# A decoder layer whose feed-forward tail writes its output feature-major, with the last permutation done by indirect DMA

## The reference, cut to what matters

```python
x = x + _L0_attn_ref(_layernorm(x), ...)    # Mamba-like block: 8 groups, 128 heads of 64, inner width 8192
x = x + _L0_xattn_ref(_layernorm(x), ctx)   # fake-quantised product: q1 (256x512) @ q2 (512x512) per sequence
x = x + _L0_ffn_ref(_layernorm(x), up, down, perm)
```

## Time and profile before

| | |
|---|---|
| time, median of 3 runs | 809.83 us (809.65 to 810.01) |
| the profiled execution | 810.87 us |
| its span in the trace | 809.0 us |
| TensorE busy | 787.9 us (97%) |
| VectorE, ScalarE, GpSimd busy | 712.9, 548.3, 589.1 us |
| DMA | 111.14 MB, mean 137 GB/s |

### The profile page before, as it was taken

One profiled execution on the slowest core, in us unless ns is written; L12 is line 12 of the kernel. 1 busy time (PEld: TensorE's weight loads), 2 busy tenths in 40 slices (PEclk: granted clock), 3 DMA queues, 4 the chain that ended last, 5 costly groups with the idle time before them and its releaser, 6 DMA issues.

```text
span 809.0 us, 14438 instructions
## 1 busy us (share of the span) xinstructions
PE 787.9 (97%) x4244; PEld 615.8 (76%) x4244; DVE 712.9 (88%) x919; ACT 548.3 (68%) x1138; POOL 589.1 (73%) x484
## 2 busy tenths in 40 slices
PE   7989999999999999999999999999999999999987
PEld 6767777777877778777887778877778777777454
DVE  6989999998998989998999989998999989998753
ACT  4777776776676776776667776766667677886242
POOL 5469777887778877797778877788778877785100
PEclk9999999999999999999999999999999999999899
DMA  7453344433443345533454244543444544521001
GB/s 234 154 201 125 125 157 170 157 117 132 169 165 118 119 156 169 169 130 104 168 169 146 101 154 155 169 155 107 144 165 156 166 166 149 184 78 40 1 1 53
DMA packets 44051, 111.14 MB, mean 137 GB/s; under 512 B 5748, under 2 KB 6644, under 8 KB 44020
## 3 DMA queue, kind: packets, MB, share of 16 engines
q1 hardware_dynamic: 44020, 110.76, 40.1%
HBM read 109.30 MB, written 1.44 MB: 137 GB/s over the span
## 4 chain that ended last, share of the span: by engine, by line
PE 93%; DVE 4%; ACT 1%; issue 1%; DMA 1%; POOL 0%; ACTq 0%; SPq 0%; DVEq 0%
PE ps_in L1309 17%; PE ps_in L1311 15%; PE ps_in L1310 15%; PE ps_y L1421 8%; PE ps_o L1309 7%; PE ps_o L1311 7%; PE ps_o L1310 7%; PE ps_y L1424 3%; PE ps_t L1383 3%; PE ps_t L1395 1%; PE ps_o L1603 1%; PE ps_t L1433 1%; PE ps_o L1549 1%; PE ps_o L1587 1%; DVE hid L1010 1%
## 5 line engine op out<-in xcount | busy, mean ns | idle before, releaser
L539 POOL TENSOR_TENSOR w_lo<-raw,w_hi 128x512 fp32r<-128x512 f32 x144 | 233.4, 1642 | 102.9 <-ACT w_hi L647 101.6
L1309 PE MATMUL ps_in<-h_hi,w_hi 128*128 128x512 f32 x560 | 226.3, 404 | 2.8 <-DVE gate L1029 2.8
L1311 PE MATMUL ps_in<-h_hi,w_lo 128*128 128x512 f32 x560 | 219.6, 392 | 0.0
L1310 PE MATMUL ps_in<-h_lo,w_hi 128*128 128x512 f32 x560 | 218.4, 390 | 0.0
L702 ACT ACTIVATE e<-e,nag 128x256 f32<-128x256 f32 (+1 forms) x512 | 183.6, 444 | 2.9 <-DVE nag L1080 2.9
L1010 DVE SCALAR_TENSOR_TENSOR hid<-ps_in,curc,hid 128x510 f32<-128x510 f32 x183 | 136.0, 743 | 4.4
L1309 PEld LDWEIGHTS ps_in<-h_hi,w_hi 128*128 128x128 f32 x560 | 105.1, 188 | 33.2 <-issue 10.5
L1311 PEld LDWEIGHTS ps_in<-h_hi,w_lo 128*128 128x128 f32 x560 | 105.4, 188 | 23.3
L570 POOL TENSOR_TENSOR e<-e,gm 128x512 f32<-128x512 f32 x64 | 100.5, 1570 | 30.8 <-DVE gm L1054 26.8
L1310 PEld LDWEIGHTS ps_in<-h_lo,w_hi 128*128 128x128 f32 x560 | 105.5, 188 | 20.4
L667 ACT ACTIVATE hid<-ps_in,curc 128x512 f32<-128x512 f32 x61 | 47.4, 777 | 102.9 <-PE ps_in L1311 102.7
(11 more groups left out here) (236 smaller groups left out, 1239.7 us busy)
## 6 DMA issues: line engine op xcount, KB each, us to landing
e<-acs_rows SPq DMA_DIRECT2D x64, 768.0 KB, 4.4
raw<-in_w_in SPq DMA_DIRECT2D x144, 256.0 KB, 4.7
rawo<-in_w_out SPq DMA_DIRECT2D x64, 256.0 KB, 3.7
craw<-in_ctx SPq DMA_DIRECT2D x8, 256.0 KB, 4.1
res<-in_x SPq DMA_DIRECT2D x4, 256.0 KB, 3.6
out_x<-res SPq DMA_DIRECT2D x4, 256.0 KB, 2.2
acs_rows<-z SPq DMA_DIRECT2D x3, 128.0 KB, 2.0
rawo<-in_w_dt SPq DMA_DIRECT2D x1, 256.0 KB, 4.5
```

The costliest lines, as they stand in the source:

```text
L539: pool.tensor_tensor(w_lo[:, slot, :], raw[:, slot, :], w_hi[:, slot, :].bitcast(F32), ALU.subtract).then_inc(s_lo, 1)
L1309: pe.matmul(dst, lh, rh, start=first, stop=False)
L1310: pe.matmul(dst, lh, rl, start=False, stop=False)
L1311: return pe.matmul(dst, ll, rh, start=False, stop=last)
```

## The change

The output tensor becomes feature-major (512 features, 512 tokens); the host turns it when it is read. The parts:

1. The permutation back and the `put` matrices are gone. The residual is turned to feature-major in the tail by 16 transposes on TensorE, copied to SBUF by ScalarE, stored to a DRAM tensor `x2_rows` by SyncE, and its rows are gathered in permuted order by four indirect DMAs that GpSimd issues. VectorE adds each down result, straight from PSUM, to the gathered rows, and GpSimd scatters the sum to the output with four more indirect DMAs.
2. At the end of the main stage the token sums are parted, the output products are taken by token tile, the square of the last tile is made before its high part, and the one-hot matrices are built later (four in place of eight).
3. The layernorm statistics are taken tile by tile, their ends in pairs.
4. The second rounding instruction moves from VectorE to ScalarE, which also sums the rows by its accumulator, in place of the 16 small products. Three of the four final normalisations move to ScalarE as well.
5. The rank-one term is a product with 128 rows, of which 127 are zero. The column sums are made with 128 columns of ones. `keep_busy` is called once, for 8 products, in place of 18 and 20.
6. The last two permuted banks are made between the up products, and the split of the permuted banks is done by VectorE alone.

The diff, cut to its core:

```diff
-WARM_A, WARM_B = 18, 20
+WARM_B = 8
+    x2_dram = nc.dram_tensor("x2_rows", [D, TOK], F32, kind="Internal").ap()
+        x2_turned = [raw[:, RAW_RING - DK + k, :] for k in range(DK)]
+        x2_rows = [rawo[:, 0, :], rawo[:, 1, :], z[:, 0, :], z[:, 1, :]]
 # SyncE
-            for t in range(TT):
-                sp.wait_ge(s_store, t + 1)
-                sp.dma_start(out[t * P:(t + 1) * P, :], res[:, t, :]).then_inc(s_out, 16)
-            sp.wait_ge(s_out, 16 * TT)
+            for k in range(DK):
+                sp.wait_ge(s_xk, k + 1)
+                sp.dma_start(x2_dram[k * P:(k + 1) * P, :], x2_turned[k]).then_inc(s_xs, 16)
+            sp.wait_ge(s_out, 16 * DK)
 # GpSimd
+            pool.wait_ge(s_perm, 32)
+            pool.wait_ge(s_xs, 16 * DK)
+            for k in range(DK):
+                pool.indirect_dma_start(x2_rows[k], None, x2_dram[:, :],
+                                        bass.IndirectOffsetOnAxis(ap=perm_col_i[:, k:k + 1], axis=0))\
+                    .then_inc(s_xg, 16)
+            for k in range(DK):
+                pool.wait_ge(s_store, k + 1)
+                pool.indirect_dma_start(out[:, :], bass.IndirectOffsetOnAxis(ap=perm_col_i[:, k:k + 1], axis=0),
+                                        x2_rows[k], None).then_inc(s_out, 16)
 # ScalarE
-            z_high_and_square(last_m, CT - 1)
+            square(last_m, CT - 1)
+            z_high(last_m, CT - 1)
...
+            def norm_keep(t):
+                act.wait_ge(s_rn, t + 1)
+                act.activation(q1[:, t, :], e1[:, t, :], ACT.Identity, bias=offset[:, :],
+                               accum_out=rowsum[:, t:t + 1]).then_inc(s_q1, 1)
+            column_sums(0)
+            column_sums(1)
+            norm_scale(0)
+            norm_scale(1)
+            norm_keep(0)
+            norm_keep(1)
             act.wait_ge(s_q1t, 1)
-            act.activation(q1T[:, 0, :, :], ps_y[:, :]..., ACT.Copy).then_inc(s_q1a, 1)
+            act.activation(q1T[:, 0, 0:2, :], ps_y[:, :]..., ACT.Copy).then_inc(s_q1a, 1)
+            norm_scale(2)
+            norm_scale(3)
+            norm_keep(2)
+            norm_keep(3)
             act.wait_ge(s_q1t, 2)
...
+            normalise(0)
+            normalise(1)
+            finish_residual(0)
+            finish_residual(1)
+            normalise(2)
+            finish_residual(2)
             act.wait_ge(s_ft, 1)
+            act.activation(f_hi[:, 0, :], feature_bank(0), ACT.Copy).then_inc(s_fhi, 1)
+            act.activation(f_hi[:, 1, :], feature_bank(1), ACT.Copy).then_inc(s_fhi, 1)
+            finish_residual(3)
+            act.activation(f_hi[:, 2, :], feature_bank(2), ACT.Copy).then_inc(s_fhi, 1)
+            act.activation(f_hi[:, 3, :], feature_bank(3), ACT.Copy).then_inc(s_fhi, 1)
+            act.wait_ge(s_xt, 1)
             for k in range(DK):
-                act.wait_ge(s_p, k + 1)
-                act.activation(p_hi[:, k, :], feature_bank(k), ACT.Copy).then_inc(s_phi, 1)
+                act.activation(x2_turned[k], out_bank(k), ACT.Copy).then_inc(s_xk, 1)
 # VectorE
+            add_attention(0)
+            add_attention(1)
+            moments(front)
+            add_attention(2)
+            quant_scales(front)
+            dve.wait_ge(s_oin, 4)
+            add_output(3)
             round_norm(0)
+            dve.wait_ge(s_of, TT * GROUPS)
+            statistics(3)
             round_norm(1)
+            moments(back)
+            one_hot(0)
+            quant_scales(back)
+            dve.wait_ge(s_q1t, 1)
+            dve.tensor_copy(q1T[:, 0, 2:4, :], ps_in[:, 0, :]...).then_inc(s_q1v, 1)
             round_norm(2)
             round_norm(3)
+            one_hot(1)
             add_product(0)
             add_product(1)
+            moments(front)
             add_product(2)
+            norm_terms(front)
+            dve.wait_ge(s_q1, TT)
+            dve.tensor_scalar(rowq[:, :], rowsum[:, :], qd[:, 6:7], qd[:, 7:8], ALU.subtract, ALU.mult)...
             add_product(3)
+            moments(back)
+            one_hot(2)
+            one_hot(3)
+            norm_terms(back)
+            dve.tensor_scalar(e1[:, 3, :], res[:, 3, :], mv[:, 3, 0:1], rstd[:, 3:4],
+                              ALU.subtract, ALU.mult).then_inc(s_fv, 1)
...
+                dve.wait_ge(s_p, k + 1)
+                step_of(dve.tensor_copy(p_hi[:, k, :], feature_bank(k)))
                 dve.tensor_tensor(p_lo[:, k, :], feature_bank(k), p_hi[:, k, :].bitcast(F32), ALU.subtract)\
                    .then_inc(s_plo, 1)
+            dve.wait_ge(s_xg, 16 * DK)
             for k in range(DK):
                 dve.wait_ge(s_dn, k + 1)
-                step_of(dve.tensor_copy(f_hi[:, k, :], src))
-                dve.tensor_tensor(f_lo[:, k, :], src, f_hi[:, k, :].bitcast(F32), ALU.subtract).then_inc(s_dlo, 1)
+                dve.tensor_tensor(x2_rows[k], x2_rows[k], feature_bank(k), ALU.add).then_inc(s_store, 1)
 # TensorE
             out_tile(last_m, CT - 3)
-            out_tile(last_m, CT - 2)
-            last_token_sums()
-            out_tile(last_m, CT - 1)
+            last_token_sums(sqsum)
+            last_out_part(CT - 2, 0)
+            last_out_part(CT - 2, 1)
+            last_token_sums(sq).then_inc(s_ss, 1)
+            last_out_part(CT - 1, 0).then_inc(s_oin, 1)
+            last_out_part(CT - 1, 1).then_inc(s_oin, 1)
+            for t in (2, 3):
+                last = last_out_part(CT - 2, t)
+                last_out_part(CT - 1, t).then_inc(s_oin, 1)
...
+            turn_q1(0)
+            turn_q1(1)
+            product(0)
+            product(1)
+            turn_q1(2)
+            turn_q1(3)
+            product(2)
+            product(3)
+            keep_busy(ps_in[:, 0, :], WARM_B)
+            turn_features(0)
+            turn_features(1)
+            pe.wait_ge(s_px, TT)
+            turn_residual(0)
+            turn_residual(1)
+            turn_features(2)
+            turn_features(3).then_inc(s_ft, 1)
+            turn_residual(2)
...
+            take_part(0, f_hi)
+            turn_residual(3).then_inc(s_xt, 1)
+            take_part(0, f_lo).then_inc(s_p, 1)
+            take_features(1)
+            pe.wait_ge(s_xk, DK)
             up_pair(0)
             up_pair(1)
-            for k in range(1, DK):
-                up_pair(2 * k)
-                up_pair(2 * k + 1)
-                down_product(k - 1)
-            down_product(DK - 1)
-            for k in range(DK):
-                for t in range(TT):
-                    put_back(k, t)
+            take_features(2)
+            up_pair(2)
+            up_pair(3)
+            take_features(3)
+            up_pair(4)
+            up_pair(5)
+            down_product(0)
+            down_product(1)
+            up_pair(6)
+            up_pair(7)
+            down_product(2)
+            down_product(3)
```

More of the change, by code:

```diff
@@ L1202, in _, with statistics, add_attention, moments @@
             z_low(last_m, CT - 1)
-            for k in range(DK):
-                one_hot(k)
             mean_square(last_m)
-            def variance(tiles):
+            dve.wait_ge(s_r, GROUPS)
+            def statistics(t):
+                dve.bn_stats(stats[:, t, :], res[:, t, :]).then_inc(s_v, 1)
+                chain[0] += 1
+            def add_attention(t):
+                dve.wait_ge(s_oin, t + 1)
+                add_output(t)
+                dve.wait_ge(s_of, TT * last_m + t + 1)
+                statistics(t)
+            def moments(two):
                 dve.wait_ge(s_v, chain[0])
-                for t in tiles:
+                for t in range(two.start, two.stop):
                     dve.bn_aggr(mv[:, t, :], stats[:, t, :]).then_inc(s_v, 1)
@@ new lines, in add_product @@
+            def add_product(t):
+                dve.wait_ge(s_pr, t + 1)
+                dve.scalar_tensor_tensor(res[:, t, :], out_bank(t), qd[:, 4:5], res[:, t, :],
+                                         ALU.mult, ALU.add).then_inc(s_px, 1)
+                dve.wait_ge(s_px, t + 1)
+                statistics(t)
+            front, back = slice(0, 2), slice(2, 4)
+            add_attention(0)
[3 more added lines that the diff above has]
+            quant_scales(front)
@@ L1435, in token_sums, with last_token_sums @@
                 last.then_inc(s_ss, 1)
-            def last_token_sums():
-                pe.wait_ge(s_tf, STEPS)
-                pe.wait_ge(s_sqs, (CT - 1) * GROUPS - 1)
-                pe.wait_ge(s_sq, STEPS)
+            def last_token_sums(part):
                 for t in range(TT):
-                    for part in (sqsum, sq):
-                        last = pe.matmul(ps_t[:, t:t + 1], part[:, t * P:(t + 1) * P], ones[:, :],
-                                         start=(part is sqsum), stop=(part is sq))
-                last.then_inc(s_ss, 1)
+                    last = pe.matmul(ps_t[:, t:t + 1], part[:, t * P:(t + 1) * P], ones[:, :],
```

(22 more changed lines are left out.)

244 lines of the change are left out of this document (113 added, 131 removed).

## The result

| | before | after |
|---|---|---|
| median (lowest to highest), 4 runs each | 809.92 us (809.65 to 811.56) | 797.47 us (795.63 to 799.65) |
| profiled execution: time | 810.87 us | 799.65 us |
| its span | 809.0 us | 797.9 us |
| mean granted clock of the span | 0.991 | 0.995 |

The changed kernel takes 1.6% less: the ratio is 0.9836 with a 95% interval of 0.9812 to 0.9859, clear of no change, though under 2%, and the medians are 12.45 us apart. The forecast was 798.8 us. A second measurement of the same kernel gave a median of 798.62 us and a ratio of 0.9846 (0.981 to 0.9883).

What follows compares the result with a forecast made beforehand. Bound taken: the chain of waits in the last 65 us, almost all TensorE, with VectorE behind the fillers. Steps sum to -11.05 us; 809.83 - 11.05 = 798.8 us, range 795.5 to 803.5.

Steps and rivals of the forecast that it cites:

- A: Token sums to the output product's first add: six output products moved behind, no one-hots ahead of mean_square; -1.7 us.
- B: First add to first Relu: three add-and-statistics pairs in place of four adds and four statistics; -0.95 us more.
- C: First Relu to last tile turned: half the rounding leaves VectorE, -1.85 us; ScalarE's accumulator costs +0.4 us.
- D: Last tile turned to first gelu: 7.5 us where today 10.3, two permuted banks ahead of the up pair; -2.8 us.
- E: First gelu to last down product: two banks between up pairs, 12.7 us where today 10.2; +2.5 us.
- F: Last down product to last add: one add of 0.7 us replaces the putting back and its tail; -7.95 us.
- G: Last add to end: GpSimd issues the last store, taken as 1.3 us; +1.3 us, bounds 0 and +2.3.
- The signs at the end: Expected milestones, within a microsecond: first add 749.0, Relu 754.5, tile turned 771.5, gelu 779.0, last gelu 790.6, last add 792.4.
- The first rival: Behind 779.6 GpSimd's eight DMAs bound the end: span 786.3 + 8c, time 815.1 us at c = 3.5, slower; chance 6%.
- own case: The prediction's main case for the whole tail: its steps hold, 798.8 us, with 796.5 to 801; chance 56%.
- The clock: Rival: with fewer fillers the clock falls to 1.2 GHz in the products or banks 0 and 1; 802.8 us; chance 18%.
- The DMA price of the page: GpSimd-issued DMA at the end: 2.0 us plus bytes over 436 GB/s, 2.6 us for 256 KB; 0.4 us less gain.

## Why the prediction was right, and where it was off

The forecast was 798.8 us; the two measurements gave 797.47 and 798.62, both in the range of 795.5 to 803.5. The sum said -11.05 against a tail shorter by 12.72, of which 1.1 us lie at the end of the trace of before and are not shown to be the change's. By its steps, each as the difference of two lines of the table:

| step | predicted | measured |
|---|---|---|
| A, first add | -1.7 | -1.91 |
| B, first Relu | -0.95 | -1.12 |
| C, last tile turned, with the accumulator | -1.85 + 0.4 | -2.11 |
| D, first gelu | -2.8 | -2.86 |
| E, last down product | +2.5 | +1.65 |
| F, last add | -7.95 | -7.90 |
| G, end | +1.3 | +1.53 |
| sum | -11.05 | -12.72 |

- **A to D** held within 0.3 us except for the accumulator. Its row sums cost 0.19 us each, beside a rounding of 0.71 (in place of the 0.8 that was taken from the Relu), and step C shows nothing of them: from the start of one rounding to the next it is 0.81 us with the sums (757.22 to 758.03), no more than the Relu that stood in for it, so the +0.4 were not there. That this is what cancelled is worked out and not tested. Doing the same on VectorE costs 1.37 us at that point.
- **E was the term of the sum that was mis-sized most**, by 0.85 us; C with its accumulator follows with 0.66. The stepping took 0.9 us for an up pair, but its row, `785.37 0.92 PE ps_o L1587 x11`, is two pairs (eleven of their twelve instructions), which ran side by side, each head in its own 32 rows of the array. Before, four of the other six pairs waited for one gelu each and ran one by one, and two overlapped in part. Now a bank or eight down products stand ahead of each two pairs; both halves of `ps_o` are free, or nearly, when that is done, and the two pairs overlap. Busy time of the up products from the first gelu to the last down product, before and after (windows of L1587 in the kernel before and of L1705 in the changed one: us, TensorE busy, its weight loads busy, granted clock, DMA share, GB/s):

```profile
786.31:796.53 10.22, 5.01 (x36) 2.91 (x36) 1.00 0.00 0
779.93:791.79 11.86, 3.37 (x36) 2.02 (x36) 1.00 0.37 108
```

  The same 36 instructions take 1.6 us less. TensorE's waits in these stretches fell only from 10.22 - 8.93 = 1.3 us to 11.86 - 11.14 = 0.7. So of the banks' 3.6 us (4.1 as they are recorded), more came back through pairs that overlap than through waits that were filled. How much of the 0.85 is the row misread can't be said, since the stepping isn't written out.
- **F** was right to 0.05 us: the last add is released by TensorE.
- **G was right in size by luck, and wrong in its working.** Its own price for an indirect DMA, c = 1.3, was measured as 1.25 us. But the step added c to the 3.83 us of the kernel before, as if the last scatter would follow the last add. It follows three other scatters. The store landed at 38.16 us of the ruler (the text's 779.6 is 38.21); then came 0.89 us to the first gather, 1.25 for each, and 3.67 from issue to landing in place of the 2.2 that the earlier trace rows give for a store. The last gather landed at 46.73, the text's 787.0 being 45.6. That is ahead of the last down product, as forecast, but VectorE did wait for a DMA (3.28 us, the sign that the text had named against itself), because the first two adds could have gone earlier. The first add released four scatters at 1.3 us each, and these ended the span. From the last add to the end it is 5.36 us: 2.40 for a lone store, 1.2 more for a scatter, 1.8 of queue. The text had 3.83 + 1.3 = 5.13. It left out the queue, and its 3.83 held 1.4 us more than a lone store, 0.3 for four in a row and 1.1 that the same stores did not take when they were run again. Two errors of opposite sign left +1.53 for +1.3.
- **The signs at the end.** First add, first Relu, last tile turned and first gelu came within a microsecond of the text (0.2, 0.3, 0.6 and 0.7 us early by the ruler). The last gelu's end (47.66 for 49.2) and the last add's end (49.53 for 51.0) were 1.5 us early, outside the microsecond that it had allowed.
- **The first rival** (GpSimd's DMAs are the bound) is what the chain shows, with nothing of its loss. "Hidden for c up to 1.9" compared the gathers with the last add alone. By the rival's own formula, 786.3 + 8c passes the forecast's 796.2 + c at c = 1.4; with the landing 1.5 us longer that is at 1.2, below the measured 1.25. So the bound was already there, 0.35 us above the own case by the formula; the semaphores, which take it away, showed 1.7. It passes the time of before only with far dearer DMAs: four extra gathers cost 5.0 us, and there are 12.7 to lose.
- **The clock** stayed at 1.00 where the text had put 18% on a fall, and not because of the fillers, which bring nothing. What held it hangs on the residual's turning: with its 16 transposes gone it fell. The Trainium skill, "TensorE: Matmul & The Clock Gate", section "Part 4: PE-mode transpose", says that transposes do not count as busy in the same way; by that rule the transposes should have held nothing. Here the windows of the run without fillers and of the run without the residual's transposes speak against it, with 1.00 and 0.50; whether these transposes run in the mode that the page means, the traces don't say. The transposes are shown to matter; that they would hold the clock alone, with no products between, isn't.
- **The DMA price of the page** was kept out of the sum. Like the row's 2.2 it was too low, but nearer. By the Trainium skill, "DMA: Bandwidth & Descriptors", section "Anatomy of one DMA", a DMA of this size is estimated at 2.6 us; a gather here took 3.67 from the start of its instruction on GpSimd to its landing. That is 0.95 on GpSimd and 2.7 behind it, near the page's figure if the engine's own time is left out of it.

## What to carry to other kernels

When data goes to memory and back on one queue to replace products, count the whole queue, loads and stores, against the moment at which its first item could go, and give each item its own semaphore: here the common wait cost 1.7 us. Don't add to a baseline such as "3.83 us from the last add to the end" before you know what is in it: a lone store took 2.40, the same four stores in another run 2.72, and only one trace showed 3.83. When a stage alternates between two engines, look at what runs side by side: putting a bank between two up pairs cost less than the bank, because the two pairs behind it then overlapped. And when TensorE's work is taken away, look at the granted clock of what follows: taking 16 transposes out brought the first gelu 1.7 us later, not earlier.

## What the runs showed that was not expected

- An indirect DMA of 128 rows of 2 KB holds GpSimd for 0.95 us with 0.30 between two of them, 1.20 for the first, which starts 0.84 us after its wait has ended. A gather lands 3.6 to 3.7 us after its start; the span ends 3.3 us after the start of the last scatter (54.89 - 51.58). Both are dearer than SyncE's store at 2.3 (the page's median; the last of the four took 2.82).
- The granted clock fell in three edits, each behind a different kind of work: few transposes and waits (0.50), products of one row with TensorE busy without a gap (0.74, then 0.50), and up and down products with 32 rows or columns and no full ones between (0.50). The last is no rule: the kernel before ran such a stage, in another order, at 1.00.
- The start and the main stage of the same code differ by up to 4 us between executions (739.80 to 743.76 at the same product), while the tail of the one kernel that was profiled twice repeats within 0.05. Between variants one thing behind the ruler moves by itself: the first gather starts 3.5 to 4.2 us after the issue of the residual's last store, so where the gathers bound the end, 0.3 us of tail is no difference.
- Two waits have no cause yet: ScalarE's 5.67 us ahead of a gelu while eight gathers were in GpSimd's queue, and SyncE's 1.43 us ahead of a store when the second rounding was on VectorE. Neither has the 1.1 us at the end of the trace of before.
